# Redrawing the written order of steps of an audio tower, so that like steps stand together

## The chip, the cores and the metric

The kernel runs on one core of a Trainium2 chip. The metric is the device time of one execution in microseconds (us).

## The reference

64 clips are cut into 45 patches each (16 frames of 16 features, stride 8) and go through a tower of two layers, 64 features wide. Cut to what matters:

```python
h = layernorm_affine(patches @ W.T + b)                        # tok, "lt"
h = h + causal_attention(layernorm(h)) @ Wo.T                  # 8 heads of 8, rope
x = layernorm(h); cw = top2(softmax(x @ gate_w + gate_b))      # 8 experts
h = h + sum(cw[:, e] * (gelu(x @ W1[e] + b1[e]) @ W2[e] + b2[e]) for e in range(8))
x = layernorm(h); xr, xw, xk, xv, xa, xg = [x + (shift(x) - x) * mix[i] for i in range(6)]
r, k, v = xr @ W_r, xk @ W_k, xv @ W_v                         # w, a, g: sigmoids of small products
S_t = S_(t-1) * exp(w_t) + (S kk)(kk a)^T + v_t k_t^T;  o_t = S_t r_t
h = h + (groupnorm(o) + bonus) * g @ W_o
h = h + routed_mlp(layernorm(h))                               # relu, two routed layers, out
```

The recurrence over the 45 positions is computed in closed form: masked products of r, k, kk, and the inverse of a triangular matrix, built up in four levels.

## The kernel before

The clips are held as pairs (64 features of one clip on partitions 0 to 63, of another on 64 to 127), 8 pairs to a chunk, so a chunk has 8 x 45 = 360 columns and there are four chunks, 0 to 3. Each chunk has its own part of SBUF (`arena`) and its own two banks of PSUM (`bank(c, 0)` and `bank(c, 1)`).

The work of the whole tower is cut into 437 steps, each for one chunk, and a table of text, `TABLE`, writes their order down. An entry `hid.5:01` reads: step hid, number 5 (here the expert), chunks 0 and 1. `ORDER` is that list spelled out. Each of TensorE (PE), ScalarE (ACT), VectorE (DVE) and GpSimd (POOL) runs through the same `ORDER` and issues its own part of each step, in that order. Semaphores alone tie the engines together; an engine that waits holds back all that stands behind in its list. Nothing is scheduled by a planner at build time.

The steps that are spoken of:

- `mean`, `var` (numbers 0 to 5, one layer norm each): PE multiplies by a centring matrix, ACT squares (L352), PE multiplies by a mean matrix, ACT takes Ln and Exp (L357, L360), DVE multiplies (L550). In norm 3, ahead of the recurrence, DVE adds the shift (L563, L564) and makes four of the six mixes (L567).
- `q`, `k`, `v`: projections. `s`: scores (a bf16 mask product and an fp32 product, 360 columns on the full array), row maximum and subtraction on DVE (L590, L592). `e`: Exp on ACT. `t`: four 128x128 transposes on PE, copy on ACT. `pv`: eight small products of 109 rows by 45 columns of the array, with DVE's reciprocal and product (L600, L602).
- `hid` (expert, chunk): two products on the two row halves of the array, written `64*128` by the profile, then Gelu on ACT (L402). `y`: two products on the two column halves, `128*64`, DVE multiplies (L674), POOL adds (L302). `cb`: one bf16 product on the full array, copied by ACT (L406). `cwT`, `b2`: small steps ahead of them.
- `mixes` (two more mixes), `rk`, `vw`, `aw`, `ab`, `gh`, `gg`, `kk`, `bon`, `kb`: projections, sigmoids and normalisations ahead of the recurrence. `kk` has four activations on ACT (L440 to L446).
- `m`, `vt`, `lx`, `lt`, `u`, `y2`, `z`, `w`, `o`: the recurrence, hundreds of products of 45 x 45 and 45 x 64. `ro`, `f`, `r`, `fo`: what follows.

ACT needs one table set for Ln and Exp (`var`, `e`, `top2`, `kk`), one for Gelu (`hid`), one for sigmoids and tanh (`vw`, `aw`, `ab`, `gh`). `tables()` issues a load (L339) where a step needs another set than the last. `ORDER` thus also decides how many loads there are.

Of the kernel before, what the change touches and what calls it, by code (L numbers as in the profile page):

```python
# [82 lines left out]


TABLE = """
tok.0:01 mean.0:0 tok.0:2 mean.0:1 var.0:0 tok.0:3 mean.0:2 var.0:1 mean.0:3 var.0:2 mean.1:0 var.0:3 mean.1:1 var.1:0
mean.1:2 var.1:1 mean.1:3 var.1:2 q.0:012 k.0:01 v.0:0 var.1:3 s.0:0 q.0:3 k.0:23 v.0:1 e.0:0 v.0:2 t.0:0 s.0:1 e.0:1
v.0:3 s.0:2 s.1:0 e.0:2 e.1:0 pv.0:0 s.0:3 t.0:1 s.1:1 t.1:0 e.1:1 t.0:2 pv.0:1 s.1:2 s.2:0 e.1:2 e.0:3 e.2:0 t.1:1
pv.1:0 s.2:1 pv.0:2 t.0:3 t.2:0 e.2:1 pv.1:1 s.1:3 s.3:0 e.1:3 pv.0:3 e.3:0 t.1:2 t.2:1 s.2:2 pv.2:0 t.1:3 s.3:1 e.2:2
pv.1:2 e.3:1 s.2:3 t.3:0 e.2:3 pv.2:1 s.4:0 t.2:2 t.3:1 pv.1:3 s.4:1 e.4:01 s.3:2 e.3:2 pv.2:2 t.2:3 s.3:3 pv.3:01  # L90
t.3:2 e.3:3 pv.2:3 t.4:0 s.5:0 s.4:2 e.4:2 pv.3:2 e.5:0 t.4:1 s.5:1 t.3:3 s.4:3 t.4:2 e.4:3 pv.3:3 e.5:1 s.5:2 t.4:3
s.5:3 e.5:2 pv.4:0 e.5:3 pv.4:12 t.5:0 pv.4:3 s.6:0 e.6:0 pv.5:0 t.5:1 s.6:1 t.5:23 e.6:1 s.6:2 t.6:0 pv.5:1 e.6:2
pv.5:2 s.6:3 s.7:0 t.6:1 s.7:1 e.7:0 e.6:3 t.6:2 pv.5:3 e.7:1 s.7:2 e.7:2 pv.6:0 t.6:3 pv.6:1 s.7:3 pv.6:2 t.7:0 e.7:3
pv.6:3 t.7:1 pv.7:0 t.7:2 pv.7:1 attT.0:0 pv.7:2 t.7:3 attT.0:1 pv.7:3 wo.0:0 attT.0:2 wo.0:1 attT.0:3 wo.0:2
mean.2:01 wo.0:3 var.2:0 mean.2:23 var.2:123 gate.0:0123 top2.0:0 hid.0:012 hid.1:0 hid.0:3 hid.1:123 cwT.0:012
cw2.0:0 b2.0:0 cwT.0:3 cw2.0:12 b2.0:1 cb.0:0 b2.0:2 y.0:0 cb.0:1 cw2.0:3 b2.0:3 cb.0:2 cb.1:0 y.0:1 cb.1:1 y.0:2
cb.1:2 hid.2:0 cb.0:3 hid.2:1 y.0:3 y.1:0 cb.1:3 cb.2:0 hid.2:2 y.1:1 cb.2:1 hid.2:3 hid.3:0 y.1:2 cb.2:2 hid.3:1
y.1:3 hid.3:2 y.2:0 cb.3:0 cb.2:3 y.2:1 cb.3:1 hid.4:0 y.2:2 hid.4:1 hid.3:3 y.3:0 cb.3:2 cb.4:0 y.3:1 y.2:3 cb.4:1
cb.3:3 hid.5:0 hid.4:2 hid.5:1 y.4:0 cb.5:0 hid.4:3 y.3:2 cb.4:2 y.4:1 hid.6:0 y.3:3 cb.4:3 hid.5:2 cb.5:1 y.5:0
hid.5:3 cb.6:0 y.4:2 cb.5:2 hid.6:1 y.4:3 cb.5:3 hid.6:2 hid.7:0 hid.6:3 y.5:12 cb.6:12 y.6:0 cb.7:0 hid.7:12 y.7:0  # L100
y.5:3 cb.6:3 y.6:12 hid.7:3 cb.7:12 y.7:1 mean.3:0 y.7:2 y.6:3 var.3:0 mean.3:1 cb.7:3 mixes.0:0 mean.3:2 var.3:1
mixes.0:1 y.7:3 rk.0:0 var.3:2 vw.0:0 rk.0:1 mean.3:3 mixes.0:2 aw.0:0 var.3:3 rk.0:2 ab.0:0 vw.0:1 mixes.0:3 vw.0:2
gh.0:0 aw.0:1 rk.0:3 aw.0:2 ab.0:1 gg.0:0 kk.0:0 gh.0:1 bon.0:0 vw.0:3 ab.0:2 kb.0:0 gg.0:1 aw.0:3 m.0:0 gh.0:2 kk.0:1
m.1:0 bon.0:1 vt.0:0 gg.0:2 kb.0:1 ab.0:3 kk.0:2 lx.0:0 m.0:1 lt.0:0 gh.0:3 bon.0:2 lx.1:0 m.1:1 lt.1:0 gg.0:3 lx.2:0
vt.0:1 kb.0:2 lt.2:0 lx.0:1 kk.0:3 m.0:2 lx.3:0 lt.0:1 bon.0:3 lt.3:0 m.1:2 lx.1:1 u.0:0 vt.0:2 kb.0:3 lt.1:1 y2.0:0
lx.0:2 z.0:0 m.0:3 lx.2:1 w.0:0 m.1:3 lt.2:1 o.0:0 lx.3:1 vt.0:3 lt.0:2 lx.0:3 mean.4:0 lt.3:1 lt.0:3 lx.1:2 var.4:0
u.0:1 lx.1:3 y2.0:1 lt.1:23 lx.2:2 ro.0:0 lt.2:2 mean.5:0 lx.2:3 lx.3:2 var.5:0 lt.2:3 z.0:1 f.0:0 lt.3:2 lx.3:3 w.0:1
u.0:2 lt.3:3 r.0:0 y2.0:2 u.0:3 o.0:1 y2.0:3 z.0:2 mean.4:1 z.0:3 w.0:23 var.4:1 o.0:23 mean.4:23 var.4:2 ro.0:1
var.4:3 r.1:0 mean.5:1 ro.0:2 var.5:1 ro.0:3 mean.5:2 f.0:1 mean.5:3 var.5:2 r.0:1 f.0:2 var.5:3 fo.0:0 r.0:2 f.0:3
r.1:1 r.0:3 r.1:23 fo.0:123  # L110
"""


# [1052 lines left out]
```

## Time and profile before

| | |
|---|---|
| median of 3 runs | 340.16 us (339.61 to 340.56) |
| the profiled execution | 339.59 us, span of its instructions 337.5 us |
| PE busy | 315.2 us (93% of the span) |
| DVE, ACT, POOL busy | 202.0, 205.5, 141.8 us |
| ACT table loads | 13, 16.7 us |
| granted PE clock | full, but for one slice of the 40, at some 110 us |

Every fp32 product leaves two records of a matmul in the trace, a bf16 product and a transpose one. A step of `hid` or `y` thus has 4 records, `s` one and two, `t` 4, `pv` 16. As a matmul's record overlaps the next one's, the length of a step is read as the distance from its start to the start of the next row.

### The profile page before, as it was taken

What the parts mean: (1) busy time and instruction counts of PE and PEld (TensorE: products, weight loads), DVE (VectorE), ACT (ScalarE), POOL (GpSimd) and SP (SyncE); (2) the same over time, 40 slices, a digit from 0 to 9 for tenths busy, and PEclk for the clock granted to TensorE, in tenths of its full rate; (3) what the DMA queues carried; (4) which work ended last, traced back from release to release, by engine and by line L of the source; (5) the groups of instructions that cost most, each with busy time, mean ns of one, the idle gap of its engine ahead of it and who ended that gap; (6) DMA issues with size and microseconds to landing.
All of it is one profiled execution on the core that took longest, in us unless ns stands there. A gap on an engine that the chain in (4) does not pass through costs nothing.

```text
span 337.5 us, 11772 instructions
## 1 busy us (share of the span) xinstructions
PE 315.2 (93%) x4888; PEld 206.9 (61%) x4888; DVE 202.0 (60%) x414; ACT 205.5 (61%) x386; POOL 141.8 (42%) x142
## 2 busy tenths in 40 slices
...
GB/s 242 381 57 64 58 60 61 58 64 61 6 6 60 56 56 62 55 64 56 63 33 1 0 0 2 2 2 4 6 5 4 4 5 6 4 2 2 2 26 68
DMA packets 20557, 14.89 MB, mean 44 GB/s; under 512 B 2328, under 2 KB 19352, under 8 KB 20376
## 3 DMA queue, kind: packets, MB, share of 16 engines
...
q14 instruction: 14, 0.11, 0.1%
...
## 4 chain that ended last, share of the span: by engine, by line
PE 80%; ACT 10%; DVE 7%; POOL 1%; issue 1%; POOLq 0%; DVEq 0%; ACTq 0%
PE PS L762 75%; PE PS L825 5%; ACT L339 2%; ACT arena L357 1%; ACT arena L360 1%; DVE PS L504 1%; ACT arena L402 1%; DVE arena L567 1%; DVE arena L550 1%; POOL arena L310 1%; POOL arena L312 1%; ACT arena L410 1%; ACT arena L414 1%; DVE arena L699 1%; DVE arena L755 1%
## 5 line engine op out<-in xcount | busy, mean ns | idle before, releaser
L762 PE MATMUL PS<-arena,K 128*64 128x360 f32 (+2 forms) x576 | 148.8, 504 | 12.4 <-DVE PS L504 5.3
L762 PE MATMUL PS<-arena 128*45 128x45 f32 (+6 forms) x3392 | 119.0, 219 | 3.5 <-POOL arena L312 1.6
L762 PEld LDWEIGHTS PS<-arena 128*45 128x45 f32 (+4 forms) x3392 | 99.6, 126 | 23.9 <-issue 13.8
L762 PEld LDWEIGHTS PS<-arena,K 128*64 128x64 f32 (+2 forms) x576 | 63.9, 176 | 73.0 <-issue 29.3
L302 POOL TENSOR_TENSOR arena<-arena 128x360 f32<-128x360 f32 x32 | 30.1, 953 | 58.3 <-DVE arena L674 58.2
L674 DVE TENSOR_TENSOR arena<-PS,arena 128x360 f32<-128x360 f32 x32 | 16.9, 531 | 29.8 <-PE PS L762 25.8
L402 ACT ACTIVATE arena<-PS,K 128x720 f32<-128x720 f32 x32 | 26.2, 860 | 8.7 <-PE PS L762 8.4
L550 DVE TENSOR_TENSOR arena<-PS,arena 128x360 f32<-128x360 f32 x24 | 12.7, 531 | 28.9 <-ACT arena L360 28.9
L381 ACT ACTIVATE arena<-arena 128x360 f32<-128x360 f32 x32 | 16.0, 512 | 17.0 <-DVE arena L592 16.9
L291 POOL TENSOR_TENSOR arena<-arena,K 128x360 f32<-128x360 f32 x32 | 24.1, 793 | 0.0
L328 POOL TENSOR_TENSOR arena<-arena 128x360 f32<-128x360 f32 x4 | 3.8, 952 | 44.5 <-DVE arena L558 44.5
L590 DVE TENSOR_REDUCE smax<-PS 128x8 f32<-128x360 f32 x32 | 16.9, 527 | 6.7 <-PE PS L762 6.4
L762 PEld LDWEIGHTS PS<-K,arena 128*45 128x45 f32 (+3 forms) x456 | 17.3, 129 | 5.6 <-issue 1.5
L825 PE MATMUL PS<-K,arena 128*128 128x128 f32 x128 | 19.3, 280 | 1.5 <-ACT arena L381 0.9
L762 PE MATMUL PS<-K,arena 128*45 128x64 f32 (+3 forms) x456 | 19.5, 232 | 0.8 <-DVE arena L727 0.5
L279 POOL TENSOR_TENSOR WG<-WG,K 128x2048 f32<-128x2048 f32 x4 | 15.2, 3809 | 11.5 <-DMA WG<-wr 11.5
L384 ACT COPY arena<-PS 128x360 f32<-128x360 f32 x32 | 14.3, 462 | 9.1 <-PE PS L825 9.0
L825 PEld LDWEIGHTS PS<-K,arena 128*128 128x128 f32 x128 | 14.3, 141 | 5.8 <-issue 2.2
L352 ACT ACTIVATE arena<-PS 128x360 f32<-128x360 f32 x24 | 11.0, 464 | 11.1 <-PE PS L762 10.7
L592 DVE TENSOR_TENSOR arena<-PS,smax 128x360 f32<-128x360 f32 x32 | 17.1, 534 | 1.1
L406 ACT COPY arena<-PS 128x360 f32<-128x360 f32 x32 | 14.0, 459 | 6.1 <-PE PS L762 5.3
L339 ACT ACT_TABLE_LOAD x13 | 16.7, 1283 | 1.0 <-PEq L1159 0.7
...
## 6 DMA issues: line engine op xcount, KB each, us to landing
...
```

The lines of the kernel that those rows point to most:

```text
L279: g.tensor_tensor(w, w, shared, ALU.add).then_inc(sem["wsum"], 1)
L291: g.tensor_tensor(a(c, KX_ + i * W).rearrange("q (h t) -> q h t", t=T), a(c, slot(4) + i * T, T).unsqueeze(1).broadcast_to([128, NH, T]), ...
L302: g.tensor_tensor(a(c, H_), a(c, H_), a(c, slot(3 + i % 2)), ALU.add).then_inc(sem["acc"], 1)
L339: s.preload_act_table_set(name)
L381: s.activation(pb, pb, ACT.Exp).then_inc(sem["s_exp"], 1)
L402: s.activation(halves(a(c, G_[i % 2], 2 * W)), both(c), ACT.Gelu, bias=k("b1", i, i + 1)).then_inc(sem["gelu"], 1)
L550: v.tensor_tensor(a(c, dst), bank(c, 0), a(c, sq), ALU.mult).then_inc(sem["ln_out"], 1)
L590: v.tensor_reduce(smax[:, c, :], sc, AX.X, ALU.max).then_inc(sem["s_max"], 1)
L592: v.tensor_tensor(a(c, PB_, 512).rearrange("q (h t) -> q h t", t=64)[:, :, 0:T], sc, smax[:, c, :].unsqueeze(2).broadcast_to([128, NH, T]) ...
L674: v.tensor_tensor(a(c, slot(3 + i % 2)), bank(c, 0), a(c, slot(8 + i % 2)), ALU.mult).then_inc(sem["y_mul"], 1)
L762: return nc.tensor.matmul(o, l, r, start=start, stop=stop)
L825: last = nc.tensor.transpose(bank(c, 1, 128, 128 * g), a(c, PB_ + 128 * g, 128), k("identf"))
```

## The change

Only the table is replaced; the 437 steps and all their instructions stay. Before and after, by two of its lines:

```diff
-cb.3:3 hid.5:0 hid.4:2 hid.5:1 y.4:0 cb.5:0 hid.4:3 y.3:2 cb.4:2 y.4:1 hid.6:0 y.3:3 cb.4:3 hid.5:2 cb.5:1 y.5:0
+cb.5:1 hid.7:0 hid.5:2 hid.4:3 hid.6:1 y.6:0 y.4:2 y.3:3 y.5:1 cb.5:2 cb.4:3 cb.6:1 cb.7:0 y.7:0 hid.5:3 hid.7:1
...
-y.5:3 cb.6:3 y.6:12 hid.7:3 cb.7:12 y.7:1 mean.3:0 y.7:2 y.6:3 var.3:0 mean.3:1 cb.7:3 mixes.0:0 mean.3:2 var.3:1
+hid.6:2 y.4:3 y.6:1 cb.7:1 mean.3:0 y.7:1 y.5:2 var.3:0 mean.3:1 cb.6:2 cb.5:3 var.3:1 hid.6:3 hid.7:2 mixes.0:0
```

Call a run a stretch of consecutive PE steps whose products use one shape of the array (128*128, 128*64, 64*128 and so on). The old table has 219 runs, the new one 162. In attention (`s`, `t`, `pv`) there were 28 runs of `pv` and 28 of `s` and `t`, now 16 and 16. From the first `hid` to the last `y` there were 26 runs of `y`, 18 of `hid` and 28 of others, now 16, 11 and 18, although eleven more steps of the next stage now stand among them. In both tables the number of chunks in flight is four. The file of the changed kernel is one line shorter, so its lines are those named here less one.

PE in the later part of attention, before; `KB` is the mask product of `s`, `45x18` is `pv`, `128x128` is `t`:

```order
L825 MATMUL PS<-K,arena 128x128 x4
L762 MATMUL PS<-KB 128x360
L762 MATMUL PS<-arena 128x360
L825 MATMUL PS<-K,arena 128x128 x8
L762 MATMUL PS<-KB 128x360
L762 MATMUL PS<-arena 128x360
L825 MATMUL PS<-K,arena 128x128 x4
L762 MATMUL PS<-arena 45x18 x16
L762 MATMUL PS<-KB 128x360
L762 MATMUL PS<-arena 128x360
L762 MATMUL PS<-KB 128x360
```

The same part after:

```order
L824 MATMUL PS<-K,arena 128x128 x8
L761 MATMUL PS<-KB 128x360
L761 MATMUL PS<-arena 128x360
L761 MATMUL PS<-arena 45x18 x24
L761 MATMUL PS<-KB 128x360
L761 MATMUL PS<-arena 128x360
L824 MATMUL PS<-K,arena 128x128 x4
L761 MATMUL PS<-arena 45x18 x8
L824 MATMUL PS<-K,arena 128x128 x4
L761 MATMUL PS<-KB 128x360
L761 MATMUL PS<-arena 128x360
```

`pv` stood alone or in twos and now stands also in threes (x24), and `s` and `t` stand in longer rows between.

PE in the middle of the experts, before; `64x360` is `hid`, `128x360` from `arena,K` is `y`, `128x360` with `KB` is `cb`:

```order
L762 MATMUL PS<-arena,KB 128x360
L762 MATMUL PS<-arena,K 128x360 x4
L762 MATMUL PS<-arena,K 64x360 x2
L762 MATMUL PS<-arena,KB 128x360
L762 MATMUL PS<-arena,K 128x360 x2
L762 MATMUL PS<-arena,K 64x360 x2
L762 MATMUL PS<-arena,K 128x360 x2
L762 MATMUL PS<-arena,K 64x360 x2
L762 MATMUL PS<-arena,KB 128x360 x2
L762 MATMUL PS<-arena,K 64x360 x2
L762 MATMUL PS<-arena,KB 128x360
```

The same part after:

```order
L761 MATMUL PS<-arena,K 64x360 x6
L761 MATMUL PS<-arena,KB 128x360 x3
L761 MATMUL PS<-arena,K 128x360 x6
L761 MATMUL PS<-arena,K 64x360 x4
L761 MATMUL PS<-arena,KB 128x360 x2
L761 MATMUL PS<-arena,K 128x360 x4
L761 MATMUL PS<-arena,K 64x360 x6
L761 MATMUL PS<-arena,KB 128x360 x2
L761 MATMUL PS<-arena,K 128x360 x6
L761 MATMUL PS<-arena,KB 128x360
L761 MATMUL PS<-arena,K 64x360 x6
```

`hid`, `y` and `cb` of two or three chunks stand together where they took turns one by one.

ACT between the experts and the recurrence, from the `aw` or `gg` ahead of the first `kk` on, before (L339 loads a table, L440 to L446 are `kk`, L433 `gh`, L418 to L421 `vw`):

```order
L436 COPY arena<-PS 128x360
L339 ACT_TABLE_LOAD
L440 ACTIVATE arena<-arena 128x360
L442 ACTIVATE arena<-arena 128x360
L444 ACTIVATE arena<-arena 128x360
L446 ACTIVATE arena<-arena,K 128x360
L339 ACT_TABLE_LOAD
L433 ACTIVATE arena<-PS 128x720
L418 COPY arena<-PS 128x360
L419 ACTIVATE arena<-PS 128x360
```

The same after (L338 loads a table, L439 to L445 are `kk`, L435 is `gg`, L351 the square of `mean.3:3`):

```order
L338 ACT_TABLE_LOAD
L439 ACTIVATE arena<-arena 128x360
L441 ACTIVATE arena<-arena 128x360
L443 ACTIVATE arena<-arena 128x360
L445 ACTIVATE arena<-arena,K 128x360
L435 COPY arena<-PS 128x360
L439 ACTIVATE arena<-arena 128x360
L441 ACTIVATE arena<-arena 128x360
L443 ACTIVATE arena<-arena 128x360
L445 ACTIVATE arena<-arena,K 128x360
L351 ACTIVATE arena<-PS 128x360
```

After `kk.0:0` a table was loaded and `gh.0:1` followed; now `kk.0:0` and `kk.0:1` share one load, and the square of `mean.3:3` stands behind both. ACT has 12 table loads instead of 13.

## Rows read from the trace of the kernel before

**Rows 1.** Windows: stretch, its us, busy us of each engine (records), PE clock.

```profile
5.25:39.08 33.83, 31.63 (x196) 16.88 (x196) 20.25 (x47) 20.31 (x44) 14.43 (x18) 1.00 0.46 162
39.08:94.50 55.42, 54.90 (x729) 39.41 (x731) 44.89 (x128) 29.70 (x68) 38.34 (x36) 1.00 0.18 51
...
110.00:120.00 10.00, 9.30 (x43) 5.58 (x44) 7.53 (x23) 6.65 (x9) 0.00 (x0) 0.66 0.21 60
...
112.22:172.06 59.84, 59.45 (x331) 24.24 (x331) 28.40 (x61) 43.17 (x72) 26.01 (x28) 0.96 0.21 59
172.06:208.38 36.32, 30.68 (x106) 14.82 (x104) 29.48 (x54) 32.56 (x60) 15.60 (x15) 1.00 0.01 2
208.38:235.49 27.11, 24.31 (x605) 18.48 (x604) 23.82 (x35) 20.38 (x36) 17.12 (x18) 1.00 0.01 3
```

**Rows 2.** Timeline of PE in the experts: start, us, instruction, records.

```profile
133.83 0.83 PE L762 MATMUL PS<-arena,K 128*64 128x360 f32 x4
134.59 0.33 PE L762 MATMUL PS<-arena,KB 128*128 128x360 bf16 x1
134.85 2.24 PE L762 MATMUL PS<-arena,K 64*128 64x360 f32 x12
137.02 0.33 PE L762 MATMUL PS<-arena,KB 128*128 128x360 bf16 x1
...
145.97 1.43 PE L762 MATMUL PS<-arena,K 128*64 128x360 f32 x8
147.33 0.48 PE L762 MATMUL PS<-arena,KB 128*128 128x360 bf16 x2
147.74 2.84 PE L762 MATMUL PS<-arena,K 64*128 64x360 f32 x16
150.51 0.33 PE L762 MATMUL PS<-arena,KB 128*128 128x360 bf16 x1
```

**Rows 3.** Timeline of PE in attention.

```profile
70.13 0.66 PE L825 MATMUL PS<-K,arena 128*128 128x128 f32 x4
70.62 0.32 PE L762 MATMUL PS<-KB 128*128 128x360 bf16 x1
...
71.39 0.60 PE L825 MATMUL PS<-K,arena 128*128 128x128 f32 x4
71.82 0.32 PE L762 MATMUL PS<-KB 128*128 128x360 bf16 x1
...
72.58 0.60 PE L825 MATMUL PS<-K,arena 128*128 128x128 f32 x4
73.11 0.52 PE L762 MATMUL PS<-arena 109*45 109x18 f32 x16
73.57 0.33 PE L762 MATMUL PS<-KB 128*128 128x360 bf16 x1
...
83.31 0.86 PE L762 MATMUL PS<-arena 109*45 109x18 f32 x32
84.10 0.33 PE L762 MATMUL PS<-KB 128*128 128x360 bf16 x1
```

**Rows 4.** Timeline of PE at the end of attention.

```profile
94.15 0.52 PE L762 MATMUL PS<-arena 109*45 109x18 f32 x16
94.51 1.11 PE L762 MATMUL PS<-K,arena 128*64 128x45 f32 x32
```

**Rows 5.** Timeline of PE between experts and recurrence; in brackets its idle time.

```profile
180.42 2.06 PE L762 MATMUL PS<-arena,K 128*128 128x360 f32 x6 [2.14 <-DVE arena L567]
...
206.18 2.27 PE L762 MATMUL PS<-arena,K 128*64 128x360 f32 x8 [1.46 <-ACT arena L433]
```

**Rows 6.** Costliest groups: busy us, mean ns; the first two of 172.06 to 235.49 us alone.

```profile
L339 ACT ACT_TABLE_LOAD x11 | 14.1, 1283 | 0.2
L567 DVE SCALAR_TENSOR_TENSOR arena<-arena,K 128x360 f32<-128x360 f32 x16 | 9.8, 675 | 0.1
...
L446 ACT ACTIVATE arena<-arena,K 128x360 f32<-128x360 f32 x4 | 2.4, 596 | 0.1
```

More of the change, by code:

```diff
@@ L85 @@
 TABLE = """
[L86 to L95, printed above, removed]
@@ L96 @@
-cw2.0:0 b2.0:0 cwT.0:3 cw2.0:12 b2.0:1 cb.0:0 b2.0:2 y.0:0 cb.0:1 cw2.0:3 b2.0:3 cb.0:2 cb.1:0 y.0:1 cb.1:1 y.0:2
-cb.1:2 hid.2:0 cb.0:3 hid.2:1 y.0:3 y.1:0 cb.1:3 cb.2:0 hid.2:2 y.1:1 cb.2:1 hid.2:3 hid.3:0 y.1:2 cb.2:2 hid.3:1
-y.1:3 hid.3:2 y.2:0 cb.3:0 cb.2:3 y.2:1 cb.3:1 hid.4:0 y.2:2 hid.4:1 hid.3:3 y.3:0 cb.3:2 cb.4:0 y.3:1 y.2:3 cb.4:1
-cb.3:3 hid.5:0 hid.4:2 hid.5:1 y.4:0 cb.5:0 hid.4:3 y.3:2 cb.4:2 y.4:1 hid.6:0 y.3:3 cb.4:3 hid.5:2 cb.5:1 y.5:0
-hid.5:3 cb.6:0 y.4:2 cb.5:2 hid.6:1 y.4:3 cb.5:3 hid.6:2 hid.7:0 hid.6:3 y.5:12 cb.6:12 y.6:0 cb.7:0 hid.7:12 y.7:0
@@ L101 @@
-y.5:3 cb.6:3 y.6:12 hid.7:3 cb.7:12 y.7:1 mean.3:0 y.7:2 y.6:3 var.3:0 mean.3:1 cb.7:3 mixes.0:0 mean.3:2 var.3:1
[L102 to L110, printed above, removed]
+tok.0:01 mean.0:0 tok.0:2 var.0:0 mean.0:1 tok.0:3 mean.0:2 var.0:1 mean.0:3 var.0:23 mean.1:012 var.1:0 mean.1:3
```

21 lines of the change are left out of this document (added).

## The prediction

> **What bounds the kernel now.** I read the busy times by stage first. In attention and in the experts TensorE (PE) has hardly any idle time: 55.42 less 54.90 us and 59.84 less 59.45 us [rows 1]. Between experts and recurrence it idles 5.64 and then 2.80 us, and there ACT is the busiest beside it: 32.56 of 36.32 us [rows 1]. So two things can move: how long PE takes for the same steps, and how long it waits. All steps stay, so the first seems fixed. The timeline of PE shows that it isn't.
>
> **What a change of shape costs.** Read the distances between rows in the experts [rows 2]. A `y` alone takes 134.59 - 133.83 = 0.76 us; two in a row take 147.33 - 145.97 = 1.36, so the second costs 0.60 and a run of `y` carries 0.16 on top of its steps. Two `hid` and a `y` take 137.02 - 134.85 = 2.17, less 0.76 is 1.41 for two; three and a `y` take 150.51 - 147.74 = 2.77, less 0.76 is 2.01 for three. The third costs 0.60, and a run of `hid` carries 0.21. A `cb` alone takes 0.26, two 0.41: 0.15 each and 0.11 for the run. In attention [rows 3] a `t` between two `s` takes 71.82 - 71.39 = 0.43; after a `pv` it takes 70.62 - 70.13 = 0.49, ahead of one 73.11 - 72.58 = 0.53. So a run of `s` and `t` carries 0.10 at its end and 0.01 to 0.06 at its start, 0.13 in the mean. A `pv` alone takes 73.57 - 73.11 = 0.46, two 84.10 - 83.31 = 0.79: 0.33 each and 0.13 for the run. In none of these rows does PE idle by the profile; the cost lies inside the busy time, which is why the busy shares don't show it. Waits on semaphores don't explain it, since the steps inside a run wait for semaphores just as the first does.
>
> The Trainium skill ("TensorEngine Tiling (Array Packing)", section Tiling Modes) says that changing the tiling mode, not just the tile, drains TensorE. By that rule 109*45, 128*45 and 128*64 are one mode, as column tiles come in 64 and 32 and 45 needs the 64. The trace agrees at one place: a `pv` ahead of an `attT` takes 94.51 - 94.15 = 0.36 us, near the 0.33 inside a run, though the written shape changes from 109*45 to 128*64 [rows 4]. Counted by modes there are 59 fewer runs instead of 57, and the gain below would be 0.3 us larger.
>
> **The change part by part.**
>
> 1. Runs in attention: 12 fewer of `pv` and 12 fewer of `s` and `t`: 12 x (0.13 + 0.13) = 3.1 us less PE time. PE bounds that stage with 0.5 us idle, so this comes through, if the other engines keep pace. DVE is busy 44.89 of 55.42 us there [rows 1]; of 52.3 us it would be 86% instead of 81%. Twos and threes also come to DVE at once. I give back 0.5 us.
>
> 2. Runs in the experts: 10 fewer of `y` at 0.16, 7 fewer of `hid` at 0.21, 10 fewer others at 0.11 (a `cb`) to 0.2 (a full fp32 step, for which I take the `hid` value): 1.6 + 1.5 + 1.3 = 4.4 us. ACT is busy 43.17 of 59.84 us here [rows 1]; of 55.4 us it would be 78%. The second `y` of a pair waits for a Gelu whose `hid` stands some four PE steps ahead; that holds in the new table too.
>
> 3. Elsewhere 57 - 24 - 27 = 6 fewer runs, at 0.17: 1.0 us.
>
> Together 8.5 us. The bounds: all 57 at the cheapest, 0.11, give 6.3 us; all at the dearest, 0.21, give 12.0. I take the sum by kinds, since each kind has its own row.
>
> 4. Waits between experts and recurrence. Before: 8.4 us of idle time from 172 to 235.5 us. The largest single ones are 2.14 us ahead of `rk.0:0` for DVE's mixes and 1.46 for a sigmoid of `gh` that stands behind a table load [rows 5]. I followed the new order by hand. At `rk.0:0`: PE now has two `cb`, `var.3:1`, `hid.6:3` and `hid.7:2` between `var.3:0` and `rk.0:0`, as much work as before (3 us), and the chain from `var.3:0` on is the same, ending in four mixes of 0.675 us each [rows 6]; but `var.3:1` itself waits, as ACT's square stands behind a table load. I put 0.8 and 0.5 us for 2.14. Ahead of `gh.0:0` ACT does a load, Ln and Exp of `var.3:2`, a load and `ab.0:0`: two loads of 1.283 us [rows 6] and three activations of about 0.55 us, 4.2 us, against 2.2 us of PE work queued: 1.7 us for 1.46. New is `var.3:3`: its square stands on ACT behind `kk.0:0` and `kk.0:1`, eight activations of 0.5 to 0.6 us [rows 6] and a load, about 5.8 us with a copy, and PE has some 3.5 us queued: about 2.5 us. What then follows (`gh.0:2`, `m.0:1` behind POOL) I put at 1.3, and some 1.5 us are left for small ones. That is 8.3 us against 8.4. Twelve loads instead of 13 are in this count, not beside it. The SP and POOL queues move only with the steps; POOL's additions to the routed weights stand at `s.7:3` and `lx.0` as before, and no DMA is issued elsewhere.
>
> 5. The start: before, PE idles 33.83 - 31.63 = 2.2 us from its first product to the first `t` [rows 1], mostly at the first `s` and `t`; in the new table the first mask product waits for POOL, which now does all four additions of `k` ahead of it, about 2.1 us, and I put another 0.7 us for the norms, whose steps now stand closer: 2.8 for 2.2, 0.6 us more. At `b2.0:0` a `cwT` now stands in between and hides the wait there, which is all of the idle time of the experts' stage: 0.4 us less [rows 1]. Both are estimates from the same order walked.
>
> 6. The clock. From 110 to 120 us the granted clock was 0.66 in the mean, so part of that stretch ran at 1.2 GHz of the 2.4, just after PE had waited for the gates; the first four `hid` pay for it. The gates and the first eight `hid` stand as before, so I cost this at nothing. If the low level didn't come, some 2.4 us would be gained (9.30 us busy there x (1 - 0.66) less what idles); if it came once more in the waits of point 4, as much would be lost. The stretch from 172 us had 1.00 in spite of its waits [rows 1].
>
> Sum: 339.6 us (profiled execution) - 8.5 + 0.5 - 0.1 + 0.6 - 0.4 = 331.7. The profiled execution is 0.6 us under the median of the runs shown, and such an offset is inside their spread; I forecast 331.8 us.
>
> **The rivals.**
>
> A. The gain is partly absorbed. PE becomes quicker, and DVE in attention (86%) and ACT in the experts, fed in bursts, become late: each wait is short, but there are many. If the gain of attention were lost wholly and half of point 2's, the time would be 331.8 + 3.1 - 0.5 + 2.2 = 336.6; half of that is more likely, 334.2. For it: ACT and DVE have in-order queues with two kinds of work each. Against it: only 0.5 and 0.4 us idle in these stages now. Chance 0.2.
>
> B. Slower than before. ACT's queue between experts and recurrence is the place. Gelus of `hid.6:3` to `hid.7:3` now stand among the Ln and sigmoid steps, one more load is needed for them, and `var.3:3`, with `vw.0:2`, `aw.0:2` and all of chunks 2 and 3 behind it, waits for two whole `kk`. Each chunk that is late by one load and one `kk` (1.28 + 2.2 = 3.5 us) delays the recurrence of that chunk, but PE has chunk 0's and 1's recurrence to do meanwhile. If that cover failed for all of chunks 1 to 3, it would cost 3 x 3.5 = 10.4 us: 331.8 + 10.4 = 342.2. It decides from 8.5 us of additional waits on, that is when idle time from `mean.3:0` to `m.1:2` is 17 us instead of 8.4. Chance 0.06.
>
> C. The cost of a run isn't saved: it belongs to the steps' partners and not to the change of shape, or PE has to wait for operands where it now fetches weights. Then only the waits change: 340.2 us. Against it stand four kinds of steps with the same pattern. Chance 0.04.
>
> D. The waits get fewer, not equal: the new order keeps expert work for PE beside the first mixes, so that the 8.4 us of point 4 fall to 5, or the low clock stays away. 328.5 us. Chance 0.12.
>
> **How the numbers follow.** The forecast, 331.8 with 330 to 333.5 of its own, has 0.58. A measurement of this kernel can tell about 0.3% from no change, 1 us. The range has to hold 8 in 10: I leave out B and C and the upper end of A, and take in D: 327.5 to 336. The forecast, D and A are faster, less a sliver: faster 0.90, same 0.03 (half of C and what lies between A and B), slower 0.07.
>
> **What would show it.** In the profile of the changed kernel PE should be busy some 8 us less (about 307), at the same number of records; the stage from the first `t` to the last `pv` should take about 3 us less than its 55.4, that of the experts about 4 less. A run of three `hid` should still take 2.0 us and one of three `pv` 1.1. Idle time of PE between `mean.3:0` and the recurrence should stay near 8 us, with the largest wait at `var.3:3` for ACT's square, and 12 table loads. The prediction is wrong if PE's busy time stays near 315 us (rival C), if idle time in attention or the experts exceeds 3 us (A), or if the waits of point 4 exceed 12 us (B).

## The result, and the profile after

The changed kernel takes 328.7 us (median of 4, 327.6 to 330.2), the kernel before 339.9 us beside it: a ratio of 0.967 (95% interval 0.963 to 0.971), so 11.2 us or 3.3% faster. The forecast was 331.8 us, with 327.5 to 336 as its range. The sign and the main term were right; some 3 us more came than was forecast. The time lies outside the forecast's own band of 330 to 333.5 and close to rival D's 328.5.

The first parts of the page of the changed kernel: span, busy time of each engine, and the granted clock in 40 slices.

```profile
span 326.5 us, 11771 instructions
...
PE 305.2 (93%) x4888; PEld 206.6 (63%) x4888; DVE 199.5 (61%) x414; ACT 202.2 (62%) x385; POOL 140.5 (43%) x142
...
PEclk9999999999999999999999999999999999999999
```

The number of PE's records is the same, 4888, and its busy time is 305.2 us instead of 315.2. PE's idle time fell only from 337.5 - 315.2 = 22.3 us to 326.5 - 305.2 = 21.3. Nearly all of the gain is thus time in which the profile shows PE busy with the same instructions. The busy share is 93% before and after.

The windows of the changed kernel, as in [rows 1]: first product to first `t`; first `t` to first `attT` (two `pv` come later still, in both kernels); first `hid` to `mean.3:0`; `mean.3:0` to `m.0:0`; `m.0:0` to `m.0:2`.

```profile
5.25:40.94 35.69, 33.47 (x199) 18.31 (x199) 21.53 (x48) 21.06 (x46) 17.42 (x22) 1.00 0.44 157
40.94:92.38 51.44, 51.44 (x730) 39.20 (x730) 44.73 (x129) 28.99 (x65) 35.31 (x32) 1.00 0.18 52
...
108.52:157.15 48.63, 47.12 (x299) 21.99 (x300) 25.40 (x58) 37.62 (x65) 21.24 (x24) 1.00 0.21 59
157.15:193.43 36.28, 31.42 (x120) 13.81 (x119) 25.19 (x50) 33.68 (x60) 16.83 (x17) 1.00 0.08 21
...
193.43:220.78 27.35, 24.87 (x488) 18.05 (x487) 25.18 (x39) 19.90 (x39) 19.43 (x19) 1.00 0.01 2
```

Attention takes 51.44 us without any idle time, before 55.42 with 0.52 [rows 1]; the window holds the same steps but for one `t` more and one `s` less, which is 0.3 us of the 4.0. The third window is not the same set of steps as before, since chunks 0 and 1 now leave sooner. PE idles 4.86 us from `mean.3:0` to `m.0:0` and 2.48 from there to `m.0:2`, before 5.64 and 2.80 [rows 1].

The timeline of PE of the changed kernel, with its idle time in brackets: attention, the first `hid`, the experts, and the stretch of point 4.

```profile
61.27 0.32 PE L761 MATMUL PS<-KB 128*128 128x360 bf16 x1
61.42 1.90 PE L761 MATMUL PS<-arena 128*128 128x360 f32 x50
63.25 0.66 PE L824 MATMUL PS<-K,arena 128*128 128x128 f32 x4
...
111.87 3.13 PE L761 MATMUL PS<-arena,K 64*128 64x360 f32 x16 [0.66 <-ACT arena L401]
115.85 2.65 PE L761 MATMUL PS<-K,arena 120*24 120x120 f32 x48 [0.85 <-DVE arena L655]
...
128.40 3.45 PE L761 MATMUL PS<-arena,K 64*128 64x360 f32 x20
131.78 0.48 PE L761 MATMUL PS<-arena,KB 128*128 128x360 bf16 x2
...
161.77 2.29 PE L761 MATMUL PS<-arena,K 128*128 128x360 f32 x10 [0.25 <-ACT arena L351]
164.72 2.86 PE L761 MATMUL PS<-arena,K 128*128 128x360 f32 x12 [0.67 <-DVE arena L566]
...
181.81 7.81 PE L761 MATMUL PS<-arena,K 64*128 64x360 f32 x32 [1.92 <-ACT arena L428]
191.27 2.23 PE L761 MATMUL PS<-arena,K 128*128 128x360 f32 x6 [1.65 <-ACT arena L351]
...
202.92 0.88 PE L761 MATMUL PS<-arena,K 64*128 64x360 f32 x4 [0.76 <-ACT arena L428]
...
220.78 3.48 PE L761 MATMUL PS<-arena 64*45 64x90 f32 x114 [1.28 <-POOL arena L311]
```

The row at 128.40 joins three `hid` and two `y`. It lasts 131.78 - 128.40 = 3.38 us; the prediction's runs give 3 x 0.60 + 0.21 and 2 x 0.60 + 0.16, 3.37 us. The first `y` starts at 130.41, so the three `hid` take 2.01 us, where 2.0 was forecast. In attention, x50 from 61.42 is the fp32 product of an `s` and three `pv`: 63.25 - 61.42 = 1.83 us. For 3 `pv` the prediction had 3 x 0.33 + 0.13 = 1.12, which leaves 0.71 for the product. At 191.27 stands the wait at `var.3:3` for ACT's square, 1.65 us, where 2.5 was forecast; the longest, 1.92, is ahead of `gh.0:0`. ACT has 12 table loads, as forecast.

**Where the time went.** For each kind of step, with another shape beside it or not, I took the median distance from its start to that of the next step in the trace of before, where PE doesn't idle. Summed over the order these "step lengths" give 306.5 us before and 298.0 after: 8.5 us less, the sum forecast for points 1 to 3. That is no independent proof, since both go by the same trace, but what a kernel takes beyond them, up to the end of PE's last product, shows where the rest went. Some kinds of step stand in the old order only once in a given surrounding, so the sums depend on how gaps are filled: filled in another way, the same trace gives 8.0 us less instead of 8.5, and single lines below move by up to 1.2 us. The column `again` is the changed kernel once more (an experiment, below).

| beyond step lengths, us | before | after | again | change forecast |
|---|---|---|---|---|
| first product to `mean.0:0` | 1.0 | 2.0 | 1.5 | 0 |
| `mean.0:0` to `mean.3:0` | 8.3 | 6.2 | 5.8 | +0.7 |
| `mean.3:0` to `m.0:0` | 6.8 | 6.4 | 6.4 | -0.1 with the next |
| `m.0:0` to `m.0:2` | 3.3 | 2.8 | 2.8 | |
| `m.0:2` to the end | 3.3 | 2.8 | 2.9 | 0 |
| sum (rounded apart) | 22.7 | 20.3 | 19.5 | +0.6 |

The first line varies by execution; between the two executions of the changed kernel the others repeat within 0.4 us. The 3 us over the forecast are no single find: some 0.9 less from `mean.3:0` to `m.0:2`, and 2.1 to 2.5 less ahead of it where 0.7 more had been put, in part by the clock (point 6 below). The 0.5 in the last line isn't shown: filled the other way, it is 3.4 before and 3.3 after, and the idle time behind `m.0:2` is 1.66 and 1.53 us.

### The profile page after: what moved, and what is told of

Same layout as the page of the kernel before. It is cut to its first block, busy times and chain, and to the rows that moved or that the text cites. A ratio compares the mean times of both kernels' runs of the same rounds, so it can differ in the third digit from the quotient of the medians.

```text
span 326.5 us, 11771 instructions
## 1 busy us (share of the span) xinstructions
PE 305.2 (93%) x4888; PEld 206.6 (63%) x4888; DVE 199.5 (61%) x414; ACT 202.2 (62%) x385; POOL 140.5 (43%) x142
## 4 chain that ended last, share of the span: by engine, by line
PE 65%; POOL 10%; DVE 9%; ACT 9%; issue 6%; POOLq 0%; DVEq 0%; ACTq 0%
PE PS L761 61%; POOL arena L301 5%; PE PS L824 5%; ACT L338 2%; DVE PS L503 1%; POOL arena L278 1%; DVE arena L723 1%; ACT arena L356 1%; POOL arena L322 1%; ACT arena L359 1%; POOL arena L309 1%; DVE arena L566 1%; POOL arena L317 1%; POOL arena L311 1%; ACT arena L351 1%
## 5 line engine op out<-in xcount | busy, mean ns | idle before, releaser
L761 PE MATMUL PS<-arena,K 128*64 128x360 f32 (+2 forms) x576 | 143.7, 495 | 12.4 <-DVE PS L503 5.3
L761 PE MATMUL PS<-arena 128*45 128x45 f32 (+6 forms) x3392 | 116.9, 219 | 3.3 <-POOL arena L311 1.7
L761 PEld LDWEIGHTS PS<-arena 128*45 128x45 f32 (+4 forms) x3392 | 98.4, 126 | 20.2 <-issue 11.4
L761 PEld LDWEIGHTS PS<-arena,K 128*64 128x64 f32 (+2 forms) x576 | 64.9, 173 | 72.0 <-issue 21.2
L401 ACT ACTIVATE arena<-PS,K 128x720 f32<-128x720 f32 x32 | 25.2, 864 | 1.6 <-PE PS L761 1.2
L383 ACT COPY arena<-PS 128x360 f32<-128x360 f32 x32 | 14.4, 463 | 9.4 <-PE PS L824 9.3
L733 DVE TENSOR_TENSOR arena<-PS,K 128x720 f32<-128x720 f32 x16 | 14.2, 904 | 8.8 <-PE PS L761 8.7
L761 PE MATMUL PS<-K,arena 128*45 128x64 f32 (+3 forms) x456 | 18.2, 231 | 0.9 <-DVE arena L655 0.8
L405 ACT COPY arena<-PS 128x360 f32<-128x360 f32 x32 | 13.1, 466 | 8.7 <-PE PS L761 8.7
L454 ACT ACTIVATE arena<-arena,K 128x180 f32<-128x180 f32 x16 | 6.3, 439 | 16.5 <-DVE arena L726 16.5
```

The costliest lines, as they stand in the source:

```text
L383: s.copy(a(c, PT_, 512).rearrange("q (r t) -> q r t", t=64)[:, :, 0:T], bank(c, 1, 512).rearrange("q (r t) -> q r t", t=64)[:, :, 0:T]).th ...
L401: s.activation(halves(a(c, G_[i % 2], 2 * W)), both(c), ACT.Gelu, bias=k("b1", i, i + 1)).then_inc(sem["gelu"], 1)
L733: v.tensor_tensor(x.rearrange("q j (p t) -> q j p t", t=T), pair(bank(c, 0)).unsqueeze(1).broadcast_to([128, 2, PP, T]), level.unsqueeze(2 ...
L761: return nc.tensor.matmul(o, l, r, start=start, stop=stop)
```

## The experiments

The first theory: a change between array shapes costs PE time inside its busy time, and fewer runs save it. The rival: the time comes from waits, because the new table brings chunks 0 and 1 out of the experts sooner. All kernels but `micro` and `micro2` compute the whole tower. Ratios are to the kernel before, run beside each.

**Half of the table.** `x_att` has the new order up to `top2` and the old one behind; `x_rest` the reverse. By one of their lines, against the changed kernel:

```diff
(x_att)
-hid.6:2 y.4:3 y.6:1 cb.7:1 mean.3:0 y.7:1 y.5:2 var.3:0 mean.3:1 cb.6:2 cb.5:3 var.3:1 hid.6:3 hid.7:2 mixes.0:0
+y.5:3 cb.6:3 y.6:12 hid.7:3 cb.7:12 y.7:1 mean.3:0 y.7:2 y.6:3 var.3:0 mean.3:1 cb.7:3 mixes.0:0 mean.3:2 var.3:1
(x_rest)
-s.3:2 e.3:2 s.2:3 pv.2:2 e.2:3 pv.1:3 pv.3:0 t.3:1 s.4:1 t.2:3 s.3:3 t.4:0 e.3:3 s.5:0 t.3:2 e.4:1 pv.2:3 pv.3:1 s.4:2
+pv.1:2 e.3:1 s.2:3 t.3:0 e.2:3 pv.2:1 s.4:0 t.2:2 t.3:1 pv.1:3 s.4:1 e.4:01 s.3:2 e.3:2 pv.2:2 t.2:3 s.3:3 pv.3:01
```

> The new order up to the gates and the choice of experts (new start, new attention), the old one from the first hid on; 192 runs of one array shape instead of 219. Theory 1 (each run of one shape costs PE 0.11 to 0.21 us beside its steps): PE needs 3.5 us less, the start waits some 1 us more as seen in the changed kernel: 337 us (336 to 338). Theory 2 (the gain comes from better covered waits, from chunks 0 and 1 leaving ahead, or from the clock): attention had only 0.5 us of idle time, so 340 us.

> The old order up to the choice of experts, the new one from the first hid on; 189 runs. Theory 1: PE needs 5.0 us less and the waits behind the experts are 1 us fewer: 334 us (332.5 to 335.5), and the saving of this kernel and of the other half add up to that of the whole change, 11.2 us. Theory 2: nearly the whole gain is here, 329 to 331 us.

Measured: `x_att` 335.1 us, ratio 0.984 (0.980 to 0.988), `x_rest` 333.4 us, 0.978 (0.975 to 0.981). The kernel before took 340.8 beside them, so they save 5.7 and 7.3 us, 13.0 together against 11.2 to 11.7 for the whole table. `x_rest` is where the first theory had it; `x_att` is below its 336 to 338, and the halves add up to more than the whole. Their step lengths sum to 303.0 and 301.5 us, 3.5 and 5.0 less than 306.5: 8.5 together. Beyond step lengths they take 20.8 and 22.6 us, before 22.7: the first half also loses less there, which is the part of its saving that wasn't expected. Much of it lies between the first `gate` and the first `cwT`: 12.17 us before, 10.62 in `x_att`, 11.32 in `x_rest`, 10.63 in the changed kernel. Some 0.85 us of this is the clock (point 6 below) and is counted in both halves. The profiled execution of `x_rest` is 1 us above its median, so that its waits can't be read more closely.

**Grouping alone.** `x_group` keeps the old order but for moves of at most three places (80 places differ), so that like steps stand together: 164 runs instead of 219, and the chunks leave the experts as before.

```diff
-v.0:3 s.0:2 s.1:0 e.0:2 e.1:0 pv.0:0 s.0:3
+s.0:2 s.1:0 v.0:3 e.0:2 e.1:0 pv.0:0 s.0:3
...
-e.2:1 pv.1:1 s.1:3 s.3:0 e.1:3
+e.2:1 s.1:3 s.3:0 pv.1:1 e.1:3
...
-hid.5:0 hid.4:2 hid.5:1 y.4:0 cb.5:0 hid.4:3 y.3:2 cb.4:2 y.4:1 hid.6:0 y.3:3 cb.4:3 hid.5:2
+hid.5:0 hid.4:2 hid.5:1 hid.4:3 y.4:0 y.3:2 y.4:1 cb.5:0 cb.4:2 y.3:3 hid.5:2 hid.6:0 cb.4:3
```

> The old order in which, in attention and in the experts, single steps were moved by at most three places so that like steps stand together: 164 runs instead of 219. The order within each chunk stays, all chunks leave the experts as before, 13 table loads. Theory 1: PE needs 7.5 us less, some of it given back as waits where cover shrank: 332.5 to 334.5 us. Theory 2: not faster than 339, as no chunk leaves ahead and covers only shrink.

Measured: 339.4 us, ratio 0.995 (0.993 to 0.998). This is a miss for the first theory as I had stated it (332.5 to 334.5), and by the time alone the rival would have won. The page and the timeline of `x_group` tell more:

```profile
PE 309.2 (92%) x4888; PEld 207.6 (62%) x4888; DVE 201.7 (60%) x414; ACT 203.6 (60%) x386; POOL 141.3 (42%) x142
```

```profile
44.02 0.49 PE L761 MATMUL PS<-arena 109*45 109x18 f32 x16
46.41 0.32 PE L761 MATMUL PS<-KB 128*128 128x360 bf16 x1 [1.90 <-DVE arena L584]
```

PE is busy 6.0 us less than before, so the saving is there; its idle time is 337.4 - 309.2 = 28.2 us instead of 22.3. By step lengths it saves 7.5 us (299.0) and takes 6.1 more beyond them (28.8 for 22.7), of which 5.3 lie between `mean.0:0` and `mean.3:0`. (PE's last product ends 1.4 us earlier than before, but in this execution the rest of the span behind it is 1.4 us longer, 4.36 for 2.94, so that the two spans look alike.) At 46.41 `s.0:3` waits 1.90 us for DVE's copy of `v.0:3` (L584): `v.0:3` was moved behind `s.0:2` and `s.1:0`, which before stood between the two. Moving a step to bring its like together took away what PE had to do while an operand was made.

**Taking the grouping away.** `x_ungroup` is the new order with moves of at most two places (94 places differ) that set like steps apart: 241 runs.

```diff
-cb.5:0 cb.3:2 cb.4:1 hid.3:3 hid.6:0 hid.4:2 hid.5:1 y.2:3 y.5:0 cb.6:0 cb.3:3 y.3:2
+y.3:1 cb.3:2 hid.3:3 cb.4:1 hid.6:0 hid.4:2 y.2:3 hid.5:1 y.5:0 cb.6:0 y.3:2 cb.3:3
```

> The new order in which, in attention and in the experts, single steps were moved by at most two places so that unlike steps alternate: 241 runs instead of 162. Chunks 0 and 1 still leave the experts ahead; one or two table loads more. Theory 1: PE needs 11 us more than in the changed kernel: 339.5 us (338 to 341.5). Theory 2: 329 to 331 us.

Measured: 349.2 us, ratio 1.024 (1.021 to 1.028), slower than the 338 to 341.5 expected. The page, and two entries of PE's waits (total, times, longest) of `x_ungroup`:

```profile
PE 318.3 (92%) x4888; PEld 207.1 (60%) x4888; DVE 200.8 (58%) x414; ACT 206.7 (60%) x387; POOL 140.8 (41%) x142
```

```profile
PE PS L761 <- ACT arena L405: 4.6, 6, 1.7
PE PS L761 <- ACT arena L401: 3.0, 2, 2.0
```

The step lengths sum to 309.0, 11.0 us over the new order's 298.0, and the rest is 29.3 us against 19.5 to 20.3. So of 20.5 us lost, 11.0 are shape changes, and 9 to 10 are the rest, above all waits for ACT's copies of `cb` (L405) and for Gelus (L401). These moves, too, disturbed the cover, and brought two table loads more. Some of it may be the clock: five of the six runs have a mean granted clock of 0.985 and spans of 346.6 to 348.2 us, the sixth 0.995 and 345.1. Neither experiment moved the runs without moving waits; it takes a kernel that has no waits.

**The cost of a change by itself.** `micro` leaves the tower out: PE alone runs on constants. For each pair of step kinds it does twelve of one, twelve of the other, and then twelve of each in turn.

```python
for f, g in pats:
    for _ in range(12): go(f)
    for _ in range(12): go(g)
    for _ in range(12):
        go(f); go(g)
```

> Nothing of the tower is computed: only TensorE runs, on constants, ten pairs of kinds of steps, each pair first as 12 of one kind, then 12 of the other, then 12 times one after the other, with no semaphore between them. Theory 1 (the cost belongs to the change of array shape): hid 0.605 and y 0.605 us each in rows of twelve, 1.57 for a pair of them in turn; a full fp32 step and a y 1.56, and a hid 1.61; a full fp32 step and a bf16 one 0.76 as in rows, since both have 128x128. If the tiling mode counts, not the written shape, then 128x64 and 128x45 in turn, and 128x64 with 109 rows, cost nothing extra (1.21 a pair), if the shape counts 1.5. Theory 2 (the cost is one of semaphores and operands, not of shape): every pair takes the sum of its two kinds in rows.

Windows of `micro`, of 12 pairs each: `hid` and `y` apart, then in turn; a full fp32 product and `y` apart, then in turn; full fp32 and bf16 (`cb`) apart, then in turn; `y` and its like with 45 columns (`128*45`) apart, then in turn.

```profile
19.60:34.10 14.50, 14.50 (x97) 7.90 (x96) 0.00 (x0) 0.00 (x0) 1.00 0.00 1
34.60:53.30 18.70, 18.70 (x97) 5.94 (x97) 0.00 (x0) 0.00 (x0) 1.00 0.00 1
53.30:67.80 14.50, 14.50 (x72) 7.74 (x72) 0.00 (x0) 0.00 (x0) 1.00 0.00 0
68.10:86.80 18.70, 18.70 (x75) 5.94 (x73) 0.00 (x0) 0.00 (x0) 1.00 0.00 1
...
121.00:130.10 9.10, 9.10 (x38) 5.71 (x37) 0.00 (x0) 0.00 (x0) 1.00 0.00 0
130.20:139.30 9.10, 9.10 (x38) 5.24 (x38) 0.00 (x0) 0.00 (x0) 1.00 0.00 0
160.70:175.20 14.50, 14.50 (x98) 6.49 (x96) 0.00 (x0) 0.00 (x0) 1.00 0.01 1
175.20:189.70 14.50, 14.50 (x98) 6.50 (x96) 0.00 (x0) 0.00 (x0) 1.00 0.00 1
```

The same number of instructions takes 14.50 us apart and 18.70 in turn, PE busy in all of it: 4.2 / 12 = 0.35 us for a pair of changes, with no other engine and no wait at work. Between fp32 and bf16 on the full array a change costs nothing, and between `128*64` and `128*45` neither. The medians of a pair, from start to start, in us, all at full clock (`t` is here four ordinary fp32 products of 128 columns, not transposes, and takes 0.893 instead of 0.43):

| pair | apart | in turn | cost | by the prediction's runs |
|---|---|---|---|---|
| `hid`, `y` | 1.21 | 1.562 | 0.35 | 0.21 + 0.16 = 0.37 |
| full fp32, `y` | 1.21 | 1.558 | 0.35 | 0.20 + 0.16 = 0.36 |
| full fp32, `hid` | 1.21 | 1.608 | 0.40 | 0.20 + 0.21 = 0.41 |
| `cb`, `y` | 0.758 | 1.014 | 0.26 | 0.11 + 0.16 = 0.27 |
| `t`, `pv` | 1.233 | 1.538 | 0.31 | 0.13 + 0.13 = 0.26 |
| full fp32, `cb` | 0.758 | 0.758 | 0 | not a change |
| `y`, 128 rows by 45 | 1.21 | 1.210 | 0 | a change, as written |
| `y`, 109 rows by 64 | 1.21 | 1.213 | 0 | a change, as written |

`micro2` asks the same of `pv`, again with PE alone on constants, and of a form of it with 128 rows and 64 columns (`wv`), with rows of full products between the pairs:

```diff
-pats = [(hid, y), (full, y), (full, hid), (full, cb), (cb, y), (y, narrow), (y, low), (t, pv), (pv, wv), (t, wv)]
+pats = [(pv, wv), (full, pv), (full, wv), (hid, pv), (y, pv)]
```

> Nothing of the tower is computed: only TensorE runs, on constants, with the small products of pv (109 rows, 45 columns of the array, 18 columns of data): against the same with 64 columns of the array, a full fp32 step, a hid and a y, in rows of twelve and in turn, with full fp32 steps between to hold the clock. Theory 1 (tiling mode): pv with its 64-column sister and with y in turn cost nothing extra, pv with a full step 0.2 to 0.3 us a pair, with hid 0.3. If the written shape counts, all four pairs cost 0.2 to 0.3 us extra.

Measured: a full product and a `pv` take 1.253 us in turn for 0.945 apart (0.31), `hid` and `pv` 1.256 (0.31), but `y` and `pv` 0.963 for 0.945 (0.02). The Trainium skill ("TensorEngine Tiling (Array Packing)", section Tiling Modes) says that changing the mode, not just the tile, drains TensorE; `109*45` and `128*64` then are one mode, and these distances agree, with 0.02 us for that pair and 0.31 for the others. The two pairs with `wv` ran at half clock and tell nothing here (last section).

**Moving table loads.** In the new table `var.3:2` brings a load ahead of `ab` and `gh`, and another behind it. `x_tuned` does `ab.0:01` and `gh.0:01` ahead of `var.3:2` and `mean.3:3` ahead of `kk.0:1`, for 10 loads instead of 12.

```diff
-mean.3:2 y.6:3 var.3:2 ab.0:01 cb.7:3 gh.0:01 y.7:3 mixes.0:2 gg.0:0 kk.0:0 gg.0:1 kk.0:1 mean.3:3 bon.0:0
+mean.3:2 ab.0:01 y.6:3 gh.0:01 cb.7:3 y.7:3 var.3:2 gg.0:0 kk.0:0 gg.0:1 mean.3:3 kk.0:1 mixes.0:2 bon.0:0
```

> The new order, but between experts and recurrence ab.0:0, ab.0:1, gh.0:0 and gh.0:1 stand ahead of var.3:2, and mean.3:3 ahead of kk.0:1: 10 table loads instead of 12, the square of mean.3:3 behind one kk instead of two. If the two largest waits of the changed kernel (2.0 us at gh.0:0 for a sigmoid behind two table loads, 1.8 us at var.3:3 for the square) are a matter of ACT's order, as theory 1 has it for what is left between experts and recurrence, both go and little comes in their place: 325 to 327 us. If ACT's work as a whole bounds this stretch and the waits only show where, they move on to later steps: 327.5 to 329 us.

Measured: 333.0 us, ratio 0.979 (0.975 to 0.982): slower than the changed kernel, and outside what either reading had (325 to 327, 327.5 to 329). Timelines of `x_tuned`, of PE, DVE and ACT:

```profile
187.37 2.66 PE L761 MATMUL PS<-arena,K 128*128 128x360 f32 x8 [2.54 <-DVE arena L702]
192.68 2.27 PE L761 MATMUL PS<-arena,K 128*128 128x360 f32 x4 [2.65 <-ACT arena L413]
```

```profile
184.18 2.11 DVE L566 SCALAR_TENSOR_TENSOR arena<-arena,K 128x360 f32<-128x360 f32 x4
186.20 0.59 DVE L698 SCALAR_TENSOR_TENSOR arena<-arena,K 128x360 f32<-128x360 f32 x1
186.70 0.53 DVE L702 TENSOR_SCALAR arena<-PS 128x360 f32<-128x360 f32 x1
```

```profile
187.26 0.50 ACT L443 ACTIVATE arena<-arena 128x360 f32<-128x360 f32 x1 [3.19 <-DVE arena L702]
```

I had looked at ACT's order alone. `var.3:2` has a tail on DVE, the shift and four mixes, and DVE's list is in order as well: the clamp of `kk.0:0` (L702) now stands behind the mixes of chunk 2, ACT waits 3.19 us for it and PE 2.54. From `mean.3:0` to `m.0:0` it takes 9.8 us beyond step lengths, for 6.4. Two loads less (2.6 us on ACT) were worth less than one such wait. The granted clock also fell here, to 0.54 in the mean from 192.68 to 199.23 us, and `m.0:0` took 3.17 us for 1.71; but of the six runs the one with a mean clock of 0.995 has a span of 330.7 us, inside the 330.2 to 331.2 of the others at 0.983 to 0.985, so the clock isn't what made this kernel slower.

**A second way, one step at a time, and the same kernel once more.** `x_late32` puts `ab`, `gh` and `kk` of chunks 0 and 1 ahead of `var.3:2`, which then stands behind `kb.0:0`; 10 loads too. `x_mean33` moves only `mean.3:3` by one place. `again` is the changed kernel.

```diff
(x_late32)
-mean.3:2 y.6:3 var.3:2 ab.0:01 cb.7:3 gh.0:01 y.7:3 mixes.0:2 gg.0:0 kk.0:0 gg.0:1 kk.0:1 mean.3:3 bon.0:0 kb.0:0 rk.0:2
+mean.3:2 ab.0:01 y.6:3 gh.0:01 cb.7:3 y.7:3 gg.0:0 kk.0:0 gg.0:1 kk.0:1 bon.0:0 mean.3:3 kb.0:0 var.3:2 bon.0:1 m.0:0
(x_mean33)
-gg.0:1 kk.0:1 mean.3:3 bon.0:0
+gg.0:1 mean.3:3 kk.0:1 bon.0:0
```

> The new order, but between experts and recurrence ab, gh and kk of chunks 0 and 1 stand ahead of var.3:2, and var.3:2 and its mixes behind kb.0:0, so that DVE's 3.3 us for the mixes of chunk 2 come neither ahead of kk.0:0's clamp (the 2.7 us wait of the kernel tuned before) nor ahead of gg; 10 table loads. If the waits here come from what stands ahead of whom on ACT and DVE: the waits at gh.0:0, bon.0:0 and var.3:3 go, m.0:0 starts some 3 us earlier, 326 to 328 us. Rival: chunk 2 is late instead, and PE, which has little of chunks 0 and 1 to do until m.0:1, waits at rk.0:2 or vw.0:2 for what it saved: 329 to 332 us.

> The new order with one step moved by one place: mean.3:3 ahead of kk.0:1. The square of mean.3:3 stands on ACT behind one kk instead of two, 2.1 us less. Theory 1 (ACT's order makes the wait at var.3:3): the 1.8 us there go, kk.0:1 comes 0.5 us later: 327.5 us, 1.2 us less than the changed kernel. Rival: var.3:3 is covered then, but the sigmoids and mixes behind it end when they did, as ACT has the same work: no change, 328.7 us.

> The changed kernel itself once more, beside its variants on the same chip. Both theories: 328.7 us (327.5 to 330). Its first profile had the full clock throughout; if the low clock after the gates comes and goes, this profile may have it and be up to 2.4 us longer there.

Measured: `again` 329.0 us, ratio 0.966 (0.963 to 0.970); `x_mean33` 327.4, 0.962 (0.959 to 0.965); `x_late32` 333.3, 0.978 (0.974 to 0.981), above the 326 to 328 expected and the 329 to 332 of the rival. Timelines of PE, of `x_late32` and then of `x_mean33`:

```profile
187.94 1.78 PE L761 MATMUL PS<-arena 64*45 64x90 f32 x48 [2.13 <-POOL arena L311]
193.29 3.10 PE L761 MATMUL PS<-arena 64*45 64x90 f32 x48 [3.57 <-DVE arena L726]
...
202.34 2.05 PE L761 MATMUL PS<-arena,K 128*128 128x360 f32 x6 [1.76 <-ACT arena L418]
```

```profile
180.37 4.40 PE L761 MATMUL PS<-arena,K 64*128 64x360 f32 x22 [1.92 <-ACT arena L428]
185.50 3.90 PE L761 MATMUL PS<-arena,K 128*128 128x360 f32 x12 [0.72 <-POOL arena L301]
190.59 1.48 PE L761 MATMUL PS<-arena,K 128*128 128x360 f32 x4 [1.19 <-ACT arena L413]
```

In `x_late32` the stretch to `m.0:0` is better than in the changed kernel (4.5 us beyond step lengths for 6.4) and the one to `m.0:2` far worse (9.9 for 2.8): chunk 0 is ready sooner, chunk 2 is missing as its cover. `x_mean33` has the lowest median of all, but not for the reason for which it was made: its waits to `m.0:0` sum to 3.83 us (1.92 + 0.72 + 1.19) against 3.57 (1.92 + 1.65), and from `gh.0:0` to `m.0:0` it takes 11.62 us as `again` does. From `mean.0:0` to the end of the span it is 0.7 us shorter than `again` (315.3 against 316.0), 0.5 of its 1.2 us in all lying ahead of `mean.0:0`, where the two don't differ. The intervals overlap, so it is not shown to be faster than the changed kernel.

The start of the experts, in PE's timeline of `again`:

```profile
107.59 6.80 PE L761 MATMUL PS<-arena,K 64*128 64x360 f32 x32 [0.52 <-DVE arena L633]
114.92 1.31 PE L761 MATMUL PS<-K,arena 120*24 120x120 f32 x22 [0.53 <-DVE arena L655]
```

Nine of the ten profiles of the tower have a slice of lowered clock at this place, `again` among them (0.82 and 0.84 in its windows 105:110 and 110:115); the profile of the changed kernel has none (1.00). From the first `hid` to the next step behind the eight it takes 114.92 - 107.59 = 7.33 us with the low clock and 115.85 - 108.52 = 7.33 without.

In the profile of before more was lost here. `x_group` has the same steps in the same order from the first `gate` to the first `y`. Windows from the last `gate` to the first `cwT`, of before and of `x_group`:

```profile
110.41:119.91 9.50, 8.98 (x38) 5.36 (x39) 7.08 (x22) 6.56 (x9) 0.00 (x0) 0.64 0.21 61
```

```profile
112.17:120.82 8.65, 7.72 (x39) 4.33 (x39) 6.73 (x20) 6.54 (x9) 0.00 (x0) 0.80 0.19 56
```

With a granted clock of 0.64 for 0.80 the same nine steps take 0.85 us longer, and PE is busy 1.26 us longer. The mean clock of whole executions points the same way, though it doesn't say where it fell: it is 0.989 or 0.990 in all 39 of the kernel before beside the experiments, and 0.992 to 1.000 in all ten of the changed kernel.

## Why the prediction was right, and where not

**What a change of shape costs** held. `micro` shows the cost with PE alone, within 0.05 us of the runs' values for each pair that changes the mode, and the run of five in the experts took what the runs gave. PE's busy time fell by 10.0 us for 8.5: 1.26 us more of it went to the clock in before (0.64 for 0.80) than in `x_group`. Attention took 4.0 us less for 3.1; 0.5 of it is the idle time of before and 0.3 the steps in the window. Rival C is out. The written shape was the wrong thing to count, as the prediction had left open: by modes it is 59 fewer changes.

**Points 1 to 3**, 8.5 us: the step lengths give 8.0 to 8.5. The give-back of 0.5 us for DVE in attention was not needed: DVE is busy 44.73 of 51.44 us, 87%, and PE doesn't idle at all. Rival A, the gain absorbed by many short waits, did not come in this table. It came in `x_group`, which has nearly as few runs and lost 6.1 of 7.5 us, in the main to waits. What keeps the gain in the new table is thus not in the count of runs but in how each step stands against its producers. I gave A 0.2 with the 0.5 us of idle time as reason against; for a table that groups without care that would have been far too low.

**Point 4**, waits between experts and recurrence, had its places right and one size wrong. At `rk.0:0` 0.25 + 0.67 us for 1.3; at `gh.0:0` 1.92 for 1.7; at `var.3:3` 1.65 for 2.5; at `gh.0:2` and `m.0:1` 0.76 + 0.44 for 1.3; in small ones and at `m.0:2` (1.28 of it) 1.65 for 1.5. Together the idle time is 4.86 + 2.48 = 7.3 us where I had 8.3. By distances from start to start, which also hold short waits that the profile counts as busy, the stretch carries 0.9 us less than before. The largest idle time is at `gh.0:0` and not at `var.3:3`. So a part of rival D was there as well: the waits did get fewer, though not to 5 us.

**Point 5**, the start: 0.6 us more idle time were forecast, and there are 35.69 - 33.47 = 2.2 us as before. That first stretch varies by execution: `tok.0:0` to `mean.0:0` took 4.0 us in the profile of before, 5.1 in that of after, 4.5 in `again` and 4.0 in `x_mean33`, with the same steps. The 0.4 us less at `b2.0:0` came: before PE idles 0.39 us there, now not at all. The 48.63 - 47.12 = 1.51 us that it now idles in this stage lie ahead of it, in the eight `hid` and at the first `cwT`, a stretch that takes no longer than before (point 6).

**Point 6**, the clock, was costed at nothing, and that is the term that failed, for a reason that doesn't hold: the gates and the first eight `hid` don't stand quite as before (`hid.0:012 hid.1:0 hid.0:3 hid.1:123` became `hid.0:0123 hid.1:0123`), and the low level was shorter. Some 0.85 us of the gain is the clock, by the windows of before and `x_group`. The price was too high as well. "If the low level didn't come, some 2.4 us would be gained": in the profile after it didn't come at all, and beside `again` nothing was gained. PE waits there for ACT's Gelus (0.66 us at 111.87, on L401) and at the end for DVE; with PE slower the waits are shorter, to the same 7.33 us. In before the low level cost 0.50 us from the first `gate` to the first `hid` (4.49 for 3.99 in `x_group`) and 0.36 on the eight `hid` (7.69 for 7.33); the rest of it was covered by ACT's Gelus. So D's second half, a gain by the clock, came in part. What decides how much of the low level comes isn't shown: of the twelve runs of `x_group` seven have a mean clock of 0.994 or 0.995, the others 0.985 to 0.989.

**Behind `m.0:2`** I had looked at nothing. Whether something was gained there isn't shown, as said under the table.

**By the number**, D came closest: 328.5, at a chance of 0.12. The time is inside the range because D had been taken in. The forecast itself was 3 us off: it gave back 0.5 us in attention and added 0.6 at the start, neither of which came; the waits of point 4 fell by 1.1 us for its 0.1; and the clock (0.85) and the gates (0.69) weren't in it as gains at all.

Rival B needed 8.5 us of additional waits at that place. In the changed kernel there were none. `x_late32` shows the mechanism at a smaller size: with `var.3:2` and its mixes behind `kb.0:0` it takes 7.1 us more between `m.0:0` and `m.0:2`, 1.9 less ahead of it; PE's idle time from `mean.3:0` to `m.0:2` is 3.42 + 7.27 = 10.7 us for 7.3. (There, too, the clock fell, and `m.1:0` took 3.03 us for 1.71.)

The 2 us fewer ahead of `mean.3:0` lie at four places: 0.5 us of idle time in attention, 0.39 at `b2.0:0`, 0.85 by the clock, and 0.69 from the first `gate` to the first `hid`, which take 3.99 us in `x_group` and `x_rest` with the old order there and 3.30 in `x_att` and the changed kernel with the new one.

What stays open: those in attention, at `b2.0:0` and from `mean.3:0` to `m.0:2` are read from traces; no run took one away by itself. Whether letting chunks 0 and 1 leave sooner is worth anything without the grouping isn't separated: `x_group` held that order fixed and lost cover, `x_ungroup` kept the new one and lost cover too.
